# A causal mask added by VectorE in PSUM in place of a TensorE product

## The chip, the cores and the metric

The kernel runs on one core of a Trainium2 chip. The metric is the device time of one execution in microseconds (us). Engines are named as in the profile: PE is TensorE (PEld its weight loads), DVE VectorE, ACT ScalarE, POOL GpSimd, SP SyncE.

## The reference

The reference is a transformer block with adaptive layer norm over two sequences of 1024 positions and 512 channels, in float32. The change touches the attention in it:

```python
q = (x @ Wq).reshape(b, s, H, D).transpose(0, 2, 1, 3)      # H = 32, D = 64
k = (x @ Wk).reshape(b, s, KVH, D).transpose(0, 2, 1, 3)    # KVH = 8
v = (x @ Wv).reshape(b, s, KVH, D).transpose(0, 2, 1, 3)
q, k = apply_rope(q, pos), apply_rope(k, pos)
scores = jnp.einsum('bhqd,bhkd->bhqk', q, k) / jnp.sqrt(jnp.float32(D))
causal = jnp.tril(jnp.ones((s, s), dtype=bool))
scores = jnp.where(causal[None, None], scores, jnp.finfo(x.dtype).min)
attn = jax.nn.softmax(scores, axis=-1)
out = jnp.einsum('bhqk,bhkd->bhqd', attn, v)
```

A layer norm stands in front of it; the output projection, a second layer norm and a gated feed-forward layer with ternary weights stand behind it.

## The kernel before

The kernel has four stages, one behind the other: `prologue` (layer norm), `attention`, `project_outputs` and `feed_forward`. Only `attention` is touched.

Attention runs in 8 groups, one per key-value head with its 4 query heads, and each group in 72 steps. Every product is done with operands split into a high and a low part, to keep float32 accuracy. For each sequence and each query block i of 128 queries, a head's scores against all keys up to the diagonal are one "row": `scores` writes up to 1024 columns into PSUM (two matmuls for each 512 columns, lines 641 and 642), and one more matmul (line 643) of `mask_r` by `ident_r` adds the causal mask of 0 and -1e30 to the last 128 columns, which are the diagonal block. `maximum` (VectorE, line 768) takes the negated maximum of the row, and `exponentials` (ScalarE, line 708) writes the probabilities and their sum. The probabilities are then turned tile by tile: `turn` (four 128x128 transposes on TensorE, line 651), `high` (ScalarE, line 695, writes `p_hi`), `low` (VectorE, line 760, writes `p_lo`), and two steps later `values` (lines 663 and 664) multiplies them by the values.

Query blocks are taken in pairs, a big one of 5 to 8 tiles and a small one of 4 to 1, 9 tiles together. So a pair is 9 steps with one tile each, and the 8 rows of the next pair (4 heads, big and small) are scored in steps 0, 1, 3, 4, 5, 6, 6 and 7 of the nine. Their maxima and exponentials are queued one step later, so in steps 1, 2, 4, 5, 6, 7 (two rows) and 8; steps 0 and 3 have none. The projections of the next queries, keys and values go in between: four steps of matmuls each, then the rotary products on VectorE (lines 783 and 784), a half swap by DMA, a sum on GpSimd, and casts on ScalarE (lines 729, 734, 741, 745).

Each engine's order is written out by hand: a function `step` per engine lists what the engine does in step T. The engines wait for each other by semaphores (`Events`). Scores have four PSUM banks, so `scores` waits for the exponential of a row two to four rows earlier (`ROW_FREED`); `turn` has two banks and waits for the low split of two steps before. Where the program speaks of `body.rows(T, 1)` it means the rows scored one step ago, and `body.tile(T, 0)` is this step's tile.

Of the kernel before, what the change touches and what calls it, by code (L numbers as in the profile page):

```python
# [20 lines left out]
ALU = mybir.AluOpType  # L21
# [3 lines left out]
F32R = mybir.dt.float32r  # L25
BF16 = mybir.dt.bfloat16

P = 128
B, S, E = 2, 1024, 512
T = B * S  # L30
# [297 lines left out]
def attention(nc, wq, wk, wv, consts_in, w_in, w_raw, cos, sin, mask, ident, hT_hi, hT_lo, ot_dram, rden_dram):  # L328
    with ExitStack() as ctx:
# [2 lines left out]

        w_hi = sb("w_hi", [P, CT, WN], F32R)
        w_lo = sb("w_lo", [P, CT, WN], F32R)
        ident_r = sb("ident_r", [P, P], F32R)
        mask_r = sb("mask_r", [P, P], F32R)
        rot_c = sb("rot_c", [P, 2, 512], F32)
        rot_s = sb("rot_s", [P, 2, 512], F32)
        rot_x = sb("rot_x", [P, 2, 512], F32)
# [12 lines left out]
        rd_rows = sb("rd_rows", [GQ * ST, P], F32)  # L352
        ps = ctx.enter_context(nc.psum_tensor("ps_b", [P, 8, 512], F32))

        consts_ready, pads_ready, k_scaled, whi_ready, w_ready = [sem(n) for n in (
            "consts_ready", "pads_ready", "k_scaled", "whi_ready", "w_ready")]
        s_ready, max_ready, p_ready, t_ready, phi_ready, plo_ready, pv_done = [sem(n) for n in (
            "s_ready", "max_ready", "p_ready", "t_ready", "phi_ready", "plo_ready", "pv_done")]
        o_copied, o_added = sem("o_copied"), sem("o_added")
        o_shifted, o_out = [[sem("%s%d" % (n, i)) for i in range(2)] for n in ("o_shifted", "o_out")]  # L360
        x_ready, x_used, vt_ready, khi_ready, k_ready, vhi_ready = [sem(n) for n in (
# [4 lines left out]
        block = ctx.enter_context(nc.Block())  # L366

        rows_s = Events(s_ready, [1] * RB, RB - ROWS_BEFORE)
        rows_m = Events(max_ready, [1] * RB, RB - ROWS_BEFORE)
        rows_p = Events(p_ready, [1] * RB, RB - ROWS_BEFORE)  # L370
        tiles_t, tiles_hi, tiles_lo, tiles_pv = [Events(s, [1] * STEPS, None) for s in (t_ready, phi_ready, plo_ready, pv_done)]
# [196 lines left out]

        @block.tensor
        def _(pe):  # L570
            pe.wait_ge(consts_ready, 2)
            pe.wait_ge(pads_ready, 1)

            def await_x(g, n):
# [46 lines left out]
            def scores(g, r):  # L621
                unit, _, i, h, _, k = row_of(r)
                first = (r // 8 + 1) % 4
                if k == 0 and first == 0:
                    for n in ([7, 9, 10] if unit == 0 else [0, 2, 3]):
                        if X_USES[n][0] == "kv":
                            kv_lo.await_(pe, g, KV.index(n))
                            kv_hi.await_(pe, g, KV.index(n))
                        else:
                            q_place[buf_of(n)].await_(pe, g, QBUF[buf_of(n)].index(n))  # L630
                if k == 0 and first == 2:
                    for n in ([11, 12] if unit == 0 else [4, 5]):
                        buf = buf_of(n)
                        q_place[buf].await_(pe, g, QBUF[buf].index(n) - (len(QBUF[buf]) if unit == 0 else 0))
                rows_p.await_(pe, g, r - ROW_FREED[k])
                nk = (i + 1) * P
                q = q_hl[:, h, i * P:(i + 1) * P]
                for k0 in range(0, nk, 512):
                    n = min(512, nk - k0)
                    bank = S_BANK + ROW_BANK[k] + k0 // 512  # L640
                    pe.matmul(ps[:, bank, 0:n], q, k_hh[:, unit, k0:k0 + n], start=True, stop=False)  # L641
                    ins = pe.matmul(ps[:, bank, 0:n], q, k_l0[:, unit, k0:k0 + n], start=False, stop=(k0 + n < nk))  # L642
                pe.matmul(ps[:, bank, n - P:n], mask_r[:], ident_r[:], start=False, stop=True).then_inc(s_ready, 1)  # L643

            def turn(g, T):
                unit, parity, i, j, column, block_ = tile_of(T)
# [39 lines left out]
        @block.scalar  # L686
        def _(act):
            act.wait_ge(consts_in, 48)
            act.copy(ident_r[:], ident[:]).then_inc(consts_ready, 1)
            act.copy(mask_r[:], mask[:]).then_inc(consts_ready, 1)  # L690

            def high(g, T):
                tiles_t.await_(act, g, T)
                tiles_pv.await_(act, g, T - P_RING)
                act.copy(p_hi[:, T % P_RING, :], ps[:, T_BANK + T % 2, :]).then_inc(phi_ready, 1)  # L695

            def copy_out(g, n):
                pair, small = divmod(n, 2)
                tiles_pv.await_(act, g, 9 * pair + (8 if small else BIG[pair % 4]))
                blocks_out[n % 2].await_(act, g, n // 2 - 1)  # L700
                act.copy(o_sb[:, n % 2, :], ps[:, O_BANK, :]).then_inc(o_copied, 1)  # L701

            def exponentials(g, r):
                unit, parity, i, h, column, k = row_of(r)
                rows_m.await_(act, g, r)
                nk = (i + 1) * P
                s = ps[:, S_BANK:S_BANK + 4, :].rearrange("p b c -> p (b c)")[:, ROW_BANK[k] * 512:ROW_BANK[k] * 512 + nk]
                act.activation(p_32[:, parity, h, column * P:column * P + nk], s, ACT.Exp, bias=negm[:, k:k + 1], scale=1.0,  # L708
                               accum_out=den[:, unit, h, i:i + 1]).then_inc(p_ready, 1)

            def step(body, T):
                if body.split(T, W_HIGH):
                    splits_in.await_(act, body.g, 0)
                    k_cols = w_raw[:, :, GQ * D:GQ * D + D]
                    act.activation(k_cols, k_cols, ACT.Copy, scale=D ** -0.5).then_inc(k_scaled, 1)
                    splits_scaled.await_(act, body.g, 0)
                    uses_x.await_(act, body.g, X_HERE - 1)
                    act.copy(w_hi[:], w_raw[:]).then_inc(whi_ready, 1)
                for g, t in body.tile(T, 0):
                    high(g, t)  # L720
                for g, n in body.blocks(T, LAG):
                    copy_out(g, n)
                for g, r in body.rows(T, 1):
                    exponentials(g, r)
                for g, n, _ in body.uses(T, 4, kinds=("kv",)):
                    buf = buf_of(n)
                    uses_x.await_(act, g, n)
                    await_buffer(act, g, n)
                    act.copy(rot_c[D:P, buf, :], ps[D:P, X_BANK, :]).then_inc(vt_ready, 1)
                for g, n, _ in body.uses(T, 1, kinds=("v",)):  # L730
                    unit = X_USES[n][1]
                    uses_x.await_(act, g, n)
                    tiles_pv.await_(act, g, (36 if unit == 0 else 0) - 1)
                    act.copy(v_hl[:, unit, :, 0:D],
                             ps[:, X_BANK, :].rearrange("p (t d) -> p t d", d=D)).then_inc(vhi_ready, 1)
                for g, n, _ in body.uses(T, 8, kinds=("kv",)):
                    _, unit, part, _ = X_USES[n]
                    buf_sum[part].await_(act, g, BUF[part].index(n))
                    rows_s.await_(act, g, 23 if unit == 0 else (55 if n == X_BODY - 1 else 55 - RB))
                    for rows in half:  # L740
                        act.copy(k_hh[rows, unit, kv_cols(part)], rot_c[0:D, part, :]).then_inc(khi_ready, 1)
                for g, n, _ in body.uses(T, 8, kinds=("qx", "qy")):
                    buf = buf_of(n)
                    buf_sum[buf].await_(act, g, BUF[buf].index(n))
                    act.copy(rot_s[:, buf, :].bitcast(F32R), rot_c[:, buf, :]).then_inc(qhi_ready[buf], 1)
                for g, d in body.dens(T, 0):
                    dens_turned.await_(act, g, d)
                    dens_out.await_(act, g, d - 1)
                    act.copy(rd_rows[:], ps[0:GQ * ST, X_BANK, 0:P]).then_inc(rd_copied, 1)

            bodies(act, step)
# [3 lines left out]
        def _(dve):  # L755
            dve.wait_ge(consts_in, 48)

            def low(g, T):
                tiles_hi.await_(dve, g, T)
                dve.tensor_tensor(p_lo[:, T % P_RING, :], ps[:, T_BANK + T % 2, :], p_hi[:, T % P_RING, :].bitcast(F32),  # L760
                                  ALU.subtract).then_inc(plo_ready, 1)

            def maximum(g, r):
                _, _, i, _, _, k = row_of(r)
                rows_s.await_(dve, g, r)
                nk = (i + 1) * P
                s = ps[:, S_BANK:S_BANK + 4, :].rearrange("p b c -> p (b c)")[:, ROW_BANK[k] * 512:ROW_BANK[k] * 512 + nk]
                dve.tensor_reduce(negm[:, k:k + 1], s, AX.X, ALU.max, negate=True).then_inc(max_ready, 1)  # L768

            def rotary_products(g, n):  # L770
# [15 lines left out]
            def step(body, T):  # L786
                for g, n, _ in body.uses(T, 4, kinds=("kv", "qx", "qy")):
                    await_buffer(dve, g, n)
                    rotary_products(g, n)
                for g, r in body.rows(T, 1):  # L790
                    maximum(g, r)
                for g, n, _ in body.uses(T, 1, kinds=("v",)):
                    unit = X_USES[n][1]
                    v_high.await_(dve, g, V.index(n))
                    dve.tensor_tensor(v_hl[:, unit, :, D:P], ps[:, X_BANK, :].rearrange("p (t d) -> p t d", d=D),
                                      v_hl[:, unit, :, 0:D].bitcast(F32), ALU.subtract).then_inc(x_used, 1)
                for g, t in body.tile(T, 0):
                    low(g, t)
                for g, d in body.dens(T, -1):
                    rows_p.await_(dve, g, 23 if d == 0 else 55)  # L800
                    dens_turned.await_(dve, g, d - 1)
# [727 lines left out]
```

## Time and profile before

| | us |
|---|---|
| median of 3 runs (2105.07 to 2113.36) | 2111.36 |
| the profiled execution | 2113.28 |
| its span, first to last instruction | 2111.5 |
| attention's tiles, first to last split | 1176.4 |

The time of a run has some 2 us around the span. The profile gives each engine's busy time, what ended its idle time ("<-" and the releasing engine and line), and the granted TensorE clock, where 1.00 is 2.4 GHz and a mean between 0.5 and 1 is a mixture with 1.2 GHz. Durations of neighbouring instructions on one engine overlap in their ends, so the step from one start to the next is what an instruction costs in its queue. Line numbers are those of the kernel before.

### The profile page before, as it was taken

Reading aid. Unit: us, or ns where it says so; the run is one execution under the profiler, and the core shown is the slowest. Engines: PE = TensorE matmul, PEld = TensorE weight load, DVE = VectorE, ACT = ScalarE, POOL = GpSimd, SP = SyncE. Lnnn points to the kernel's source line nnn. Section 1 sums busy time; section 2 is a strip of 40 time slices with the busy share of each in tenths; the row PEclk is TensorE's granted clock in tenths of the full one; section 3 lists DMA queues with packets and bytes.
Section 4 is the critical chain, followed back from the end, with each engine's and each line's share of the span. In section 5 each row is a group of like instructions: output and inputs, shape, how many; then the busy total and the mean of one; then the engine's idle time right before and its main releaser. Section 6 shows DMA issues by size and latency. Waiting matters only on the chain. (4 is left out here: it accounts for less than half of the span.)

```text
span 2111.5 us, 30964 instructions
## 1 busy us (share of the span) xinstructions
PE 1808.2 (86%) x9601; PEld 1499.0 (71%) x9601; DVE 1408.7 (67%) x1935; ACT 1161.6 (55%) x2283; POOL 796.9 (38%) x532
## 2 busy tenths in 40 slices
PE   4679999999999999999999999357766669999997
PEld 4458878878878887787788888245555547777776
DVE  5347777767767777767777777487797946454543
ACT  1137777767767777677677678343343334232221
POOL 0023333333333333333333332175665714444443
PEclk9789999999999999999999999778888889999999
DMA  6033233233233333323332332667577510101000
GB/s 236 6 79 75 58 98 93 58 86 89 66 77 89 80 74 81 83 73 74 95 78 64 91 73 56 173 168 175 151 184 161 146 55 1 45 1 45 1 26 20
DMA packets 161113, 178.62 MB, mean 85 GB/s; under 512 B 25265, under 2 KB 112057, under 8 KB 160961
## 3 DMA queue, kind: packets, MB, share of 16 engines
q1 hardware_dynamic: 160960, 176.64, 32.9%
q8 instruction: 89, 1.46, 0.3%
q14 instruction: 64, 0.52, 0.1%
HBM read 79.83 MB, written 25.44 MB: 50 GB/s over the span
## 5 line engine op out<-in xcount | busy, mean ns | idle before, releaser
L760 DVE TENSOR_TENSOR p_lo<-ps_b,p_hi 128x512 fp32r<-128x512 f32 x576 | 396.0, 689 | 207.2 <-ACT p_hi L695 203.0
L695 ACT CAST p_hi<-ps_b 128x512 fp32r<-128x512 f32 x576 | 338.4, 587 | 253.2 <-PE ps_b L651 247.4
L768 DVE TENSOR_REDUCE negm<-ps_b 128x1 f32<-128x640 f32 (+7 forms) x512 | 379.6, 751 | 93.6 <-PE ps_b L643 89.7
L708 ACT ACTIVATE p<-ps_b,negm 128x640 f32<-128x640 f32 (+7 forms) x512 | 382.3, 749 | 67.9 <-DVE negm L768 63.3
L651 PE MATMUL ps_b<-ident,p 128*128 128x128 f32 x2304 | 352.8, 276 | 14.4 <-issue 8.7
L641 PE MATMUL ps_b<-k_hh,q_hl 128*128 128x512 f32 (+3 forms) x768 | 267.7, 349 | 16.8 <-DMA q_hl<-rot_x 12.1
L651 PEld LDWEIGHTS ps_b<-ident,p 128*128 128x128 f32 x2304 | 251.3, 141 | 41.4 <-issue 13.8
L663 PE MATMUL ps_b<-p_hi,v_hl 128*128 128x512 f32 x576 | 275.8, 479 | 1.7 <-ACT o_sb L701 1.3
L822 POOL TENSOR_TENSOR rot_c<-rot_c,rot_x 128x512 f32<-128x512 f32 (+1 forms) x96 | 123.3, 1285 | 358.1 <-DMA rot_x<-rot_s 358.1
L642 PE MATMUL ps_b<-k_l,q_hl 128*128 128x512 f32 (+3 forms) x768 | 257.0, 347 | 0.0
L977 PE MATMUL ps_c<-wo_hi,o_hi 128*128 128x512 f32 x256 | 120.4, 470 | 139.3 <-DVE o_lo L1115 139.3
L664 PE MATMUL ps_b<-p_lo,v_hl 128*128 128x512 f32 x576 | 227.9, 396 | 0.0
L817 POOL TENSOR_TENSOR o_sb<-o_sb,o_low 64x512 f32<-64x512 f32 x128 | 163.9, 1283 | 147.1 <-DMA o_low<-o_sb 147.0
L1268 PE MATMUL ps_d<-h_hi,gu 128*128 128x512 f32 x512 | 201.3, 393 | 7.8 <-ACT xn_d L1287 4.6
L1269 PE MATMUL ps_d<-h_lo,gu 128*128 128x512 f32 x512 | 200.0, 391 | 0.0
L599 PE MATMUL ps_b<-hT_hi,w_hi 128*128 128x512 f32 x384 | 157.1, 409 | 38.5 <-DVE w_lo L805 13.2
L641 PEld LDWEIGHTS ps_b<-k_hh,q_hl 128*128 128x128 f32 x768 | 145.1, 189 | 57.9 <-issue 16.9
L977 PEld LDWEIGHTS ps_c<-wo_hi,o_hi 128*128 128x128 f32 x256 | 57.9, 226 | 159.0 <-DVE o_lo L1115 90.4
L642 PEld LDWEIGHTS ps_b<-k_l,q_hl 128*128 128x128 f32 x768 | 145.4, 189 | 28.0
L600 PE MATMUL ps_b<-hT_hi,w_lo 128*128 128x512 f32 x384 | 153.6, 400 | 0.0
L601 PE MATMUL ps_b<-hT_lo,w_hi 128*128 128x512 f32 x384 | 152.2, 396 | 0.0
L1436 DVE TENSOR_TENSOR a<-ps_d,sg 128x512 f32<-128x512 f32 x64 | 44.2, 691 | 158.5 <-PE ps_d L1269 140.8
(141 smaller groups left out, 3420.9 us busy)
## 6 DMA issues: line engine op xcount, KB each, us to landing
rot_x<-rot_s SPq DMA_DIRECT2D x320, 64.0 KB, 2.0
q_hl<-rot_s SPq DMA_DIRECT2D x128, 128.0 KB, 2.3
q_hl<-rot_x SPq DMA_DIRECT2D x128, 128.0 KB, 2.4
o_low<-o_sb SPq DMA_DIRECT2D x128, 128.0 KB, 2.2
attention_out<-o_sb SPq DMA_DIRECT2D x128, 128.0 KB, 2.5
o_raw<-attention_out SPq DMA_DIRECT2D x32, 512.0 KB, 4.9
rd<-attention_out SPq DMA_DIRECT2D x64, 256.0 KB, 9.0
wf<-in_L_ffn_w_gate_up SPq DMA_DIRECT2D x16, 512.0 KB, 11.6
```

What stands on the lines that cost most here:

```text
L641: pe.matmul(ps[:, bank, 0:n], q, k_hh[:, unit, k0:k0 + n], start=True, stop=False)
L642: ins = pe.matmul(ps[:, bank, 0:n], q, k_l0[:, unit, k0:k0 + n], start=False, stop=(k0 + n < nk))
L651: ins = pe.transpose(ps[:, T_BANK + T % 2, h * P:(h + 1) * P], p_32[:, parity, h, column * P:(column + 1) * P], ident[:])
L663: pe.matmul(ps[:, O_BANK, :], v_hl[:, unit, j, :], p_hi[:, T % P_RING, :], start=(j == 0), stop=False)
L664: pe.matmul(ps[:, O_BANK, :], v_hl[:, unit, j, :], p_lo[:, T % P_RING, :], start=False, stop=(j == i)).then_inc(pv_done, 1)
L695: act.copy(p_hi[:, T % P_RING, :], ps[:, T_BANK + T % 2, :]).then_inc(phi_ready, 1)
L708: act.activation(p_32[:, parity, h, column * P:column * P + nk], s, ACT.Exp, bias=negm[:, k:k + 1], scale=1.0, accum_out=den[:, unit, h, i ...
L760: dve.tensor_tensor(p_lo[:, T % P_RING, :], ps[:, T_BANK + T % 2, :], p_hi[:, T % P_RING, :].bitcast(F32), ALU.subtract).then_inc(plo_read ...
L768: dve.tensor_reduce(negm[:, k:k + 1], s, AX.X, ALU.max, negate=True).then_inc(max_ready, 1)
L977: pe.matmul(ps[:, i, t, :], hi, wo_hi[:, kk, :], start=(kk == 0), stop=False)
L1268: pe.matmul(ps[:, bank + half, :], gu[:, m, half, k, :], h_hi[:, parity, k, :], start=(k == 0), stop=False)
L1269: i = pe.matmul(ps[:, bank + half, :], gu[:, m, half, k, :], h_lo[:, parity, k, :], start=False, stop=(k == CT - 1))
```

## The change

The mask product on TensorE goes, with its constants `mask_r` and `ident_r`. The second score matmul of a row now ends the accumulation and signals. VectorE adds the mask to the diagonal block in PSUM (`hide_later_keys`), signals `masked`, and `maximum` waits for that signal. In VectorE's step the mask additions stand first, then the low split, and the maxima behind the low split, where they stood ahead of it. The mask constant is turned, as it is added directly now. Nothing else in any engine's order differs.

```diff
-                    ins = pe.matmul(ps[:, bank, 0:n], q, k_l0[:, unit, k0:k0 + n], start=False, stop=(k0 + n < nk))
-                pe.matmul(ps[:, bank, n - P:n], mask_r[:], ident_r[:], start=False, stop=True).then_inc(s_ready, 1)
+                    ins = pe.matmul(ps[:, bank, 0:n], q, k_l0[:, unit, k0:k0 + n], start=False, stop=True)
+                ins.then_inc(s_ready, 1)
...
-            act.copy(ident_r[:], ident[:]).then_inc(consts_ready, 1)
-            act.copy(mask_r[:], mask[:]).then_inc(consts_ready, 1)
...
+            def hide_later_keys(g, r):
+                nk, k, s = row_scores(r)
+                rows_s.await_(dve, g, r)
+                dve.tensor_tensor(s[:, nk - P:nk], s[:, nk - P:nk], mask[:], ALU.add).then_inc(masked, 1)
+
             def maximum(g, r):
-                rows_s.await_(dve, g, r)
+                nk, k, s = row_scores(r)
+                rows_masked.await_(dve, g, r)
                 dve.tensor_reduce(negm[:, k:k + 1], s, AX.X, ALU.max, negate=True).then_inc(max_ready, 1)
...
                 for g, r in body.rows(T, 1):
+                    hide_later_keys(g, r)
+                for g, t in body.tile(T, 0):
+                    low(g, t)
+                for g, r in body.rows(T, 1):
                     maximum(g, r)
...
-                for g, t in body.tile(T, 0):
-                    low(g, t)
```

On VectorE, beside a pair whose next rows are 6 and 3 tiles wide, steps 2 to 5 of the nine stood so before (`negm` is the negated maximum, `rot_c` and `rot_s` the rotary products):

```order
 L760 TENSOR_TENSOR p_lo<-ps_b,p_hi 128x512 [waits b_phi_ready] x2
 L783 TENSOR_TENSOR rot_c<-ps_b,cos 128x512 [waits b_x_ready,b_k_ready]
 L784 TENSOR_TENSOR rot_s<-ps_b,sin 128x512
 L768 TENSOR_REDUCE negm<-ps_b 128x1 [waits b_s_ready]
 L760 TENSOR_TENSOR p_lo<-ps_b,p_hi 128x512 [waits b_phi_ready]
 L768 TENSOR_REDUCE negm<-ps_b 128x1 [waits b_s_ready]
 L760 TENSOR_TENSOR p_lo<-ps_b,p_hi 128x512 [waits b_phi_ready]
```

And so they stand in the changed kernel, in the same place, from step 3:

```order
 L755 TENSOR_TENSOR p_lo<-ps_b,p_hi 128x512 [waits b_phi_ready]
 L786 TENSOR_TENSOR rot_c<-ps_b,cos 128x512 [waits b_x_ready,b_k_ready]
 L787 TENSOR_TENSOR rot_s<-ps_b,sin 128x512
 L766 TENSOR_TENSOR ps_b<-ps_b,mask 128x128 [waits b_s_ready]
 L755 TENSOR_TENSOR p_lo<-ps_b,p_hi 128x512 [waits b_phi_ready]
 L771 TENSOR_REDUCE negm<-ps_b 128x1 [waits b_masked]
 L766 TENSOR_TENSOR ps_b<-ps_b,mask 128x128 [waits b_s_ready]
 L755 TENSOR_TENSOR p_lo<-ps_b,p_hi 128x512 [waits b_phi_ready]
 L771 TENSOR_REDUCE negm<-ps_b 128x1 [waits b_masked]
```

The low split moved from behind the maximum to between the mask addition and the maximum. ScalarE's queue in the changed kernel, steps 4 to 7 of the same nine, is the same as before but for the line numbers (each CAST of `p_hi` is `high`, each ACTIVATE an exponential):

```order
 L703 ACTIVATE p,den<-ps_b,negm 128x768 [waits b_max_ready]
 L690 CAST p_hi<-ps_b 128x512 [waits b_pv_done,b_t_ready]
 L703 ACTIVATE p,den<-ps_b,negm 128x768 [waits b_max_ready]
 L690 CAST p_hi<-ps_b 128x512 [waits b_pv_done,b_t_ready]
 L703 ACTIVATE p,den<-ps_b,negm 128x384 [waits b_max_ready]
 L690 CAST p_hi<-ps_b 128x512 [waits b_pv_done,b_t_ready]
```

Nothing moved in that queue; what moved is the work that `b_max_ready` stands for.

## Rows read from the trace of the kernel before

**Rows 1.** The page: 40 slices, PE's busy tenths and granted clock.

```profile
PE   4679999999999999999999999357766669999997
...
PEclk9789999999999999999999999778888889999999
```

**Rows 2.** Stretches: length, busy PE, PEld, DVE, ACT, POOL, PEclk, DMA share, GB/s.

```profile
147.20:1323.60 1176.40, 1120.28 (x6666) 951.46 (x6663) 865.98 (x1297) 867.08 (x1905) 389.95 (x306) 1.00 0.32 78
...
1420.00:1500.00 80.00, 58.90 (x237) 45.41 (x235) 65.86 (x44) 31.39 (x32) 50.17 (x20) 0.82 0.72 174
```

**Rows 3.** Waits from 147 to 1324 us: total us, times, longest.

```profile
ACT p_hi L695 <- PE ps_b L651: 247.0, 276, 4.4
...
DVE p_lo L760 <- ACT p_hi L695: 203.0, 326, 2.2
...
DVE negm L768 <- PE ps_b L643: 77.6, 129, 3.2
...
PE ps_b L641 <- ACT p L708: 2.6, 9, 0.3
```

**Rows 4.** PE in order of time: start us, duration us, line, operation.

```profile
703.02 0.22 PE L643 MATMUL ps_b<-ident_r,mask_r 128*128 128x128 f32 x1
703.08 0.39 PE L641 MATMUL ps_b<-k_hh,q_hl 128*128 128x384 f32 x1
...
709.38 0.28 PE L643 MATMUL ps_b<-ident_r,mask_r 128*128 128x128 f32 x1
709.49 0.62 PE L651 MATMUL ps_b<-ident,p 128*128 128x128 f32 x4
```

**Rows 5.** DVE and then ACT in order of time, same columns, with idle before.

```profile
700.73 0.95 DVE L768 TENSOR_REDUCE negm<-ps_b 128x1 f32<-128x768 f32 x1
...
702.19 0.55 DVE L768 TENSOR_REDUCE negm<-ps_b 128x1 f32<-128x384 f32 x1
703.21 0.69 DVE L760 TENSOR_TENSOR p_lo<-ps_b,p_hi 128x512 fp32r<-128x512 f32 x1 [0.47 <-ACT p_hi L695]
703.82 1.01 DVE L768 TENSOR_REDUCE negm<-ps_b 128x1 f32<-128x384 f32 x2
...
701.71 0.90 ACT L708 ACTIVATE p<-ps_b,negm 128x768 f32<-128x768 f32 x1 [0.73 <-DVE negm L768]
...
702.60 0.58 ACT L695 CAST p_hi<-ps_b 128x512 fp32r<-128x512 f32 x1
703.07 0.59 ACT L708 ACTIVATE p<-ps_b,negm 128x384 f32<-128x384 f32 x1
```

**Rows 6.** DVE groups by shape, 147.2 to 1323.6 us: busy, mean ns, idle before.

```profile
L768 DVE TENSOR_REDUCE negm<-ps_b 128x1 f32<-128x512 f32 x64 | 42.5, 685 | 5.7 <-PE ps_b L643 5.1
...
L783 DVE TENSOR_TENSOR rot_c<-ps_b,cos 128x512 f32<-128x512 f32 x60 | 41.0, 683 | 0.1
...
L768 DVE TENSOR_REDUCE negm<-ps_b 128x1 f32<-128x128 f32 x60 | 16.6, 287 | 4.1 <-PE ps_b L643 1.7
```

**Rows 7.** Groups by line, same stretch, same columns.

```profile
L708 ACT ACTIVATE p<-ps_b,negm 128x896 f32<-128x896 f32 (+3 forms) x504 | 376.4, 750 | 53.9 <-DVE negm L768 49.5
L768 DVE TENSOR_REDUCE negm<-ps_b 128x1 f32<-128x896 f32 (+3 forms) x504 | 373.7, 751 | 81.3 <-PE ps_b L643 77.6
...
L643 PE MATMUL ps_b<-ident_r,mask_r 128*128 128x128 f32 x504 | 119.3, 237 | 0.0
...
L745 ACT CAST rot_s<-rot_c 128x512 fp32r<-128x512 f32 x60 | 37.2, 620 | 0.0
L741 ACT CAST k_hh<-rot_c 64x512 fp32r<-64x512 f32 x60 | 37.0, 617 | 0.7
L729 ACT COPY rot_c<-ps_b 64x512 f32<-64x512 f32 x30 | 17.5, 582 | 0.7
...
L718 ACT CAST w_hi<-w_raw 128x1536 fp32r<-128x1536 f32 x7 | 10.4, 1482 | 0.7
L734 ACT CAST v_hl<-ps_b 128x512 fp32r<-128x512 f32 x15 | 8.8, 588 | 0.0
```

More of the change, by code:

```diff
@@ L334, in attention @@
         w_lo = sb("w_lo", [P, CT, WN], F32R)
-        ident_r = sb("ident_r", [P, P], F32R)
-        mask_r = sb("mask_r", [P, P], F32R)
         rot_c = sb("rot_c", [P, 2, 512], F32)
@@ L353, in attention @@
         ps = ctx.enter_context(nc.psum_tensor("ps_b", [P, 8, 512], F32))
[L355 to L358, printed above, removed]
+        pads_ready, k_scaled, whi_ready, w_ready = [sem(n) for n in ("pads_ready", "k_scaled", "whi_ready", "w_ready")]
+        masked, s_ready, max_ready, p_ready, t_ready, phi_ready, plo_ready, pv_done = [sem(n) for n in (
+            "masked", "s_ready", "max_ready", "p_ready", "t_ready", "phi_ready", "plo_ready", "pv_done")]
         o_copied, o_added = sem("o_copied"), sem("o_added")
@@ L368, in attention @@
         rows_s = Events(s_ready, [1] * RB, RB - ROWS_BEFORE)
+        rows_masked = Events(masked, [1] * RB, RB - ROWS_BEFORE)
         rows_m = Events(max_ready, [1] * RB, RB - ROWS_BEFORE)
@@ L570, in _ @@
         def _(pe):
-            pe.wait_ge(consts_ready, 2)
             pe.wait_ge(pads_ready, 1)
@@ L761, in low, with row_scores @@
                                   ALU.subtract).then_inc(plo_ready, 1)
+            def row_scores(r):
+                _, _, i, _, _, k = row_of(r)
+                nk = (i + 1) * P
+                return nk, k, ps[:, S_BANK:S_BANK + 4, :].rearrange("p b c -> p (b c)")[:, ROW_BANK[k] * 512:ROW_BANK[k] * 512 + nk]
+            def hide_later_keys(g, r):
+                nk, k, s = row_scores(r)
+                rows_s.await_(dve, g, r)
+                dve.tensor_tensor(s[:, nk - P:nk], s[:, nk - P:nk], mask[:], ALU.add).then_inc(masked, 1)
             def maximum(g, r):
-                _, _, i, _, _, k = row_of(r)
-                rows_s.await_(dve, g, r)
-                nk = (i + 1) * P
-                s = ps[:, S_BANK:S_BANK + 4, :].rearrange("p b c -> p (b c)")[:, ROW_BANK[k] * 512:ROW_BANK[k] * 512 + nk]
+                nk, k, s = row_scores(r)
+                rows_masked.await_(dve, g, r)
                 dve.tensor_reduce(negm[:, k:k + 1], s, AX.X, ALU.max, negate=True).then_inc(max_ready, 1)
@@ L1519 @@
     arrays = {"in_" + name: np.ascontiguousarray(inputs[name]) for name in INPUTS}
-    arrays.update(in_cos=cos, in_sin=sin, in_mask=np.where(k > q, np.float32(NEG), np.float32(0)).astype(np.float32),
+    arrays.update(in_cos=cos, in_sin=sin, in_mask=np.where(k < q, np.float32(NEG), np.float32(0)).astype(np.float32),
                   in_identity=np.eye(P, dtype=np.float32))
```

## The prediction

> **What bounds the kernel now.** I first read the page's slices, to find the stage. The mask is used in the attention stage alone, where TensorE shows nine tenths and more in slice after slice at a full granted clock [rows 1]. The stretch between the first and the last split of a probability tile is 1176.4 us long, with 576 such tiles, so 2.04 us each; TensorE is busy for 1120.3 us of it, VectorE for 866.0 and ScalarE for 867.1 [rows 2]. Matmul durations overlap, so the busy time doesn't prove that TensorE is dense; the waits do. ScalarE waits 247.0 us for the transposes of TensorE, VectorE waits 203.0 us for ScalarE's split and 77.6 us for the mask product, while TensorE waits for a softmax row only 2.6 us [rows 3]. Everyone waits for TensorE. A TensorE slot saved in this stage is therefore worth its full length, as long as the other two keep their slack. Whether they keep it is the whole question.
>
> **What is removed.** 512 mask products leave TensorE (504 of them in the stretch). Their mean duration is 237 ns, but that is mostly pipeline. The start of one to the start of the next matmul is 0.06 us behind a wide score product and 0.11 us behind a 128-wide one [rows 4]. So the path gains 504 x 0.06 = 30 us to 504 x 0.11 = 55 us, no more, and not the 119 us of its busy row. The two constant casts on ScalarE and the wait for them lie ahead of the stage, under other work: nothing.
>
> The Trainium skill (TensorE: Matmul & The Clock Gate, Back-to-back issue gap) gives a warm gap of N / 2.4 + 2.5 ns, which is 56 ns for 128 columns. The first of the two slots agrees, and the estimate by it alone would be 29 us for the whole gain, 2 us short of the low end.
>
> **What is added.** 512 additions of 128x128 on VectorE, one input in PSUM. The trace has none of this size. The nearest row is the 128-wide reduction from PSUM, 287 ns; the 512-wide PSUM operation, 683 ns, is the other bound [rows 6]. I take 0.29, since the width is the same, and 0.21 us of queue, because neighbours on VectorE overlap by 0.08 (a low split of 0.69 us is followed by the next start after 0.61 [rows 5]). That is 504 x 0.21 = 106 us more VectorE work, 972 of 1176. As work it fits under TensorE.
>
> **What is moved.** This is the step that decides. For an attention step T the changed queues hold:
> ScalarE: split high(T), then the exponentials of the rows scored in step T-1, then its casts for the projections, then high(T+1).
> VectorE: mask of those rows, split low(T), then the row maxima, then step T+1.
> Before, the maxima stood ahead of low(T). A maximum ran while ScalarE did high(T), and low(T) ran under the exponential; neither queue waited for the other twice in one step. The slack is seen at 702.60: high(T) is followed by its exponential after 0.47 us, because the maximum had started at 702.19, before low(T) [rows 5].
> Now low(T) waits for high(T), the maximum stands behind low(T), the exponential waits for the maximum, and high(T+1) stands behind the exponential on ScalarE. Queued behind the waiting low split are the maximum, and through it the exponential, the next high split and the next low split. It is a ring through both engines, once per step with rows, and nothing in it overlaps.
>
> **The ring, term by term.** Eight score rows per nine steps fall in seven of them (one step has two), so the stretch has 63 x 7 = 441 steps with rows and 135 plain ones.
> 1. Start of high to start of low: 702.60 to 703.21, 0.61 us [rows 5]. 441 x 0.61 = 269 us.
> 2. Start of low to start of the maximum behind it: 703.21 to 703.82, 0.61 us [rows 5]. 269 us. The mask's own semaphore is long set, since low lies between.
> 3. Maximum to exponential: the row sum 373.7 us [rows 7] and 0.03 us of hand-over each (700.73 + 0.95 to 701.71 [rows 5]), 389 us. In 63 steps the second row's maximum hides under the first exponential; such small rows cost from 0.29 to 0.69 us [rows 6], say 0.52 with the hand-over: -33. So 356 us.
> 4. Exponential to high: row sum 376.4 us [rows 7]; the accumulator read lies inside (701.71 to 702.60 is 0.89 for one of 0.90 [rows 5]), less 0.02 each: 366 us.
> 5. Plain steps: low split 0.61 and mask 0.21 on VectorE run in series there, about 0.81. 135 x 0.81 = 109 us. Without that pairing it would be ScalarE's 0.47: 63 us.
> 6. ScalarE's other casts, 37.2 + 37.0 + 17.5 + 10.4 + 8.8 = 111 us [rows 7], stand in its queue between an exponential and the next high. Most fall behind steps with rows: 100 us. Were they all hidden: 0.
> 7. The rotary products, two of 0.68 us [rows 6] or 1.2 us of queue, hide under exponential and high, which together are longer, except directly behind a plain step (four uses a group, 32): 38 us.
> The sum is 269 + 269 + 356 + 366 + 109 + 100 + 38 = 1507 us for a stretch that took 1176: 331 us more. The mask itself lies beside the ring (VectorE waits there for high anyway) and costs nothing except in term 5; the copies of the output stand between high and the exponential, under low and the maximum.
> TensorE needs 1176 - 43 = 1133 us for its own work, which now hides under 1507. It is asked in time: a transpose needs the low split of two steps before, and a score row needs the exponential of one or two steps before, which is at least 2 us ahead of its use in the ring. Its saved slots bring nothing.
> The profiled execution took 2113.3 us around a span of 2111.5, 2 us over the median shown. 2113 + 331 = 2444, and some 6 us for the value splits, which wait for a ScalarE copy and then stand ahead of the next mask: **2450 us**, 16% slower.
>
> The Trainium skill (VectorE: DVE Perf Modes, The DRAIN you can't avoid) says that the next operation does not start until the pipe is empty. The 0.61 us above speaks against it for these operations, and the same page's section on two instructions with no wait between them allows it. With full durations of 0.69 term 2 would be an estimate of 304 us and the time some 2485.
>
> **The rivals.**
> A, faster: the ring's period stays under TensorE's. This would need the queues to overlap low(T) with an exponential of the same step, or a period below 2.04 us. For it: VectorE and ScalarE are idle a quarter of the time [rows 2], and the added work fits. Against it: one ring step with an average row is 0.61 + 0.61 + 0.77 + 0.73 = 2.7 us, and the plain steps give back only 1.2 us each, 162 us against 441 x 0.7 = 309. If it holds: 2113 less 30 to 55, **2058 to 2083**.
> B, the product's slot doesn't go away: the weight load of the transposes takes it, and A holds otherwise: **2113**.
> C, the ring closes, but its soft terms hide: 5 at 63, 6 and 7 at nothing, 1323 us in all, +147: **2260**; with half of them, 2350. For it: casts that wait for the projections might find the ring waiting anyway.
> D, TensorE can't run ahead through the plain steps. They would then cost its own 2.04 us and not 0.81: 135 x 1.23 = +166, **2610**. It decides if a transpose is late whenever two short ring steps meet. Against it: behind the low split that frees the transposes' bank the ring still has a maximum and an exponential, while TensorE needs under 1 us.
> E, the granted clock falls. TensorE is 74% busy from 1420 to 1500 us, about the share it would have in the ring, and there the clock was 0.82 [rows 2]. At such a mean 36% of the time is at 1.2 GHz, where nine steps need 2 x 18 = 36 us of TensorE against the ring's 23.9: 9 steps take 1 / (0.36 / 36 + 0.64 / 23.9) = 27 us, 1720 in all, **2660**. Against it: that stage has long waits for data, while here each wait is under 2 us, and the attention stage ran at 1.00 throughout.
>
> **How the numbers follow.** The ring as summed 0.63, C 0.10, D 0.12, E 0.08, A 0.05, B 0.02. The likeliest gives 2450. To hold 8 in 10 the range takes the ring with its bounds, the upper half of C and D: 2320 to 2630; A, B, the rest of C and most of E are left out. Faster by over 0.5% is A, 0.05; within 0.5%, which is about what a measurement here can't tell from no change, B, 0.02; slower the rest, 0.93.
>
> **What would show it.** In the changed profile the stretch of the tiles should be near 1507 us; VectorE's low split still waits for ScalarE's high; above all ScalarE's exponential should wait for the maximum some 441 times and over 1.2 us each time with big rows (49.5 us in total now [rows 7]), which is several hundred us. TensorE should wait for exponentials and low splits, hundreds of us where there are hardly any. The idle before the score reductions should be near nothing. The maximum's start should lie 0.61 us behind the low split's. The mask addition should be 0.29 us. The clock at 1.00 decides against E, and a stretch of under 1176 us with the exponential close behind high(T) would refute the ring. I am wrong in size rather than sign if transposes turn up as the releaser of high(T) behind plain steps (D), or if casts run while VectorE is the later one (C).

## The result

| | median, us | ratio to before | 95% interval |
|---|---|---|---|
| before | 2112.4 | | |
| changed | 2491.9 | 1.181 | 1.178 to 1.183 |

The change makes the kernel 18% slower: 380 us more, where 2450 us had been forecast in a range of 2320 to 2630. The loss lies in attention alone. Its tiles take 1557.8 us, from the start of the first low split to the start of the last, against 1176.4 [rows 2]; everything behind them takes 783 us, and took some 787.

The stretch of the tiles, to the end of its last split, and the rest in the changed kernel (length, then busy PE, PEld, DVE, ACT, POOL, PEclk, DMA share, GB/s):

```profile
145.10:1703.60 1558.50, 1223.54 (x6162) 957.43 (x6160) 964.12 (x1801) 865.89 (x1905) 393.93 (x307) 0.93 0.24 59
...
1703.60:2486.00 782.40, 608.21 (x2594) 483.95 (x2594) 471.48 (x501) 262.60 (x322) 387.68 (x209) 0.89 0.35 91
```

ScalarE does exactly the work that it did (865.9 us busy, 867.1 before) in 382 us more. VectorE is busy for 98 us more, with 504 mask additions. No engine is full. What fills the time is seen in the waits of the same stretch (total us, times, longest), which answer to [rows 3]:

```profile
ACT p L703 <- DVE negm L771: 633.6, 441, 3.1
DVE p_lo L755 <- ACT p_hi L690: 554.7, 458, 2.4
...
PE ps_b L638 <- ACT p L703: 145.9, 125, 3.0
...
ACT p_hi L690 <- PE ps_b L648: 45.1, 50, 3.0
PE ps_b L616 <- DVE rd_b L807: 44.9, 15, 3.6
...
ACT p_hi L690 <- PE ps_b L661: 8.4, 3, 2.9
```

ScalarE's exponentials wait for a maximum 441 times, once in every step with rows, for 634 us (49.5 before, in [rows 7]); VectorE's low split waits 555 us for ScalarE's high split. The two engines wait for each other in turn, and TensorE, for which both used to wait, waits for them: ScalarE's wait for the transposes fell from 247 to 45 us.

One step of that, ACT and then DVE in order of time (start us, duration us, line, operation, idle before):

```profile
801.74 0.58 ACT L690 CAST p_hi<-ps_b 128x512 fp32r<-128x512 f32 x1
803.67 0.69 ACT L703 ACTIVATE p<-ps_b,negm 128x512 f32<-128x512 f32 x1 [1.35 <-DVE negm L771]
804.26 0.19 ACT L703 ACTIVATION_READ_ACCUMULATOR p<-ps_b,negm 128x1 f32 x1
804.35 0.58 ACT L690 CAST p_hi<-ps_b 128x512 fp32r<-128x512 f32 x1
...
802.35 0.69 DVE L755 TENSOR_TENSOR p_lo<-ps_b,p_hi 128x512 fp32r<-128x512 f32 x1 [1.22 <-ACT p_hi L690]
802.96 0.68 DVE L771 TENSOR_REDUCE negm<-ps_b 128x1 f32<-128x512 f32 x1
803.56 0.49 DVE L766 TENSOR_TENSOR ps_b<-ps_b,mask 128x128 f32<-128x128 f32 x2
804.96 0.69 DVE L755 TENSOR_TENSOR p_lo<-ps_b,p_hi 128x512 fp32r<-128x512 f32 x1 [0.92 <-ACT p_hi L690]
```

High starts at 801.74, low at 802.35, the maximum at 802.96, the exponential at 803.67, the next high at 804.35: 0.61 + 0.61 + 0.71 + 0.68 = 2.61 us, one behind the other. The two mask additions at 803.56 lie in VectorE's idle time, under the exponential.

### The profile page after: what moved, and what is told of

Same layout as the page of the kernel before. It is cut to its first block and busy times, and to the rows that moved or that the text cites. A ratio compares the mean times of both kernels' runs of the same rounds, so it can differ in the third digit from the quotient of the medians.

```text
span 2486.4 us, 30451 instructions
## 1 busy us (share of the span) xinstructions
PE 1914.7 (77%) x9089; PEld 1505.7 (61%) x9089; DVE 1499.9 (60%) x2447; ACT 1159.9 (47%) x2281; POOL 798.9 (32%) x532
## 5 line engine op out<-in xcount | busy, mean ns | idle before, releaser
L638 PE MATMUL ps_b<-k_hh,q_hl 128*128 128x512 f32 (+3 forms) x768 | 293.5, 382 | 158.3 <-ACT p L703 147.7
L648 PE MATMUL ps_b<-ident,p 128*128 128x128 f32 x2304 | 382.1, 292 | 40.8 <-ACT rot_c L724 17.3
L690 ACT CAST p_hi<-ps_b 128x512 fp32r<-128x512 f32 x576 | 329.4, 583 | 54.9 <-PE ps_b L648 45.1
L648 PEld LDWEIGHTS ps_b<-ident,p 128*128 128x128 f32 x2304 | 291.7, 150 | 99.9 <-issue 35.7
L660 PE MATMUL ps_b<-p_hi,v_hl 128*128 128x512 f32 x576 | 294.0, 510 | 59.0 <-ACT o_sb L696 58.0
L639 PE MATMUL ps_b<-k_l,q_hl 128*128 128x512 f32 (+3 forms) x768 | 271.4, 366 | 0.0
L661 PE MATMUL ps_b<-p_lo,v_hl 128*128 128x512 f32 x576 | 239.9, 417 | 0.0
L838 POOL TENSOR_TENSOR rot_x<-rot_c,rot_s 128x512 fp32r<-128x512 f32 x64 | 82.2, 1284 | 393.2 <-ACT rot_s L740 393.2
L639 PEld LDWEIGHTS ps_b<-k_l,q_hl 128*128 128x128 f32 x768 | 155.9, 203 | 27.0
L660 PEld LDWEIGHTS ps_b<-p_hi,v_hl 128*128 128x128 f32 x576 | 118.3, 205 | 74.8 <-ACT o_sb L696 73.9
L766 DVE TENSOR_TENSOR ps_b<-ps_b,mask 128x128 f32<-128x128 f32 x512 | 142.4, 289 | 26.5 <-PE ps_b L639 25.4
```

Of the source, the lines that this page charges most:

```text
L648: ins = pe.transpose(ps[:, T_BANK + T % 2, h * P:(h + 1) * P], p_32[:, parity, h, column * P:(column + 1) * P], ident[:])
L660: pe.matmul(ps[:, O_BANK, :], v_hl[:, unit, j, :], p_hi[:, T % P_RING, :], start=(j == 0), stop=False)
L661: pe.matmul(ps[:, O_BANK, :], v_hl[:, unit, j, :], p_lo[:, T % P_RING, :], start=False, stop=(j == i)).then_inc(pv_done, 1)
```

## The experiments

Two explanations were to be told apart: the ring (the order of VectorE's queue, with the low split ahead of the maxima), and the mask's own work and wait on VectorE. After the first runs a third question came up, what the addition costs in a queue without the ring. Each edit is against the kernel that is named; ratios are to the kernel before, with 95% intervals.

### The order without the mask addition

Against the kernel before, mask product still on TensorE:

```diff
                 for g, n, _ in body.uses(T, 4, kinds=("kv", "qx", "qy")):
                     await_buffer(dve, g, n)
                     rotary_products(g, n)
+                for g, t in body.tile(T, 0):
+                    low(g, t)
                 for g, r in body.rows(T, 1):
                     maximum(g, r)
...
-                for g, t in body.tile(T, 0):
-                    low(g, t)
```

> The kernel before with its mask product on TensorE, but VectorE's maxima queued behind the low split, as in the changed kernel; no mask addition. The theory of the ring (high, low, maximum, exponential, high in series through ScalarE and VectorE) expects nearly the whole loss: the changed kernel's 2492 us less the mask's share of plain steps (126 x 0.21 = 26) and no more, so 2455 to 2500 us, with ScalarE waiting some 600 us for maxima. The rival, that the mask addition on VectorE is the cost (504 x 0.29 = 146 us of work and its wait), expects 2105 to 2160 us.

Measured: 2484.0 us, ratio 1.176 (1.170 to 1.182). The order alone brings the whole loss but for 8 us, which the two intervals don't separate; the kernel has no addition on VectorE at all. The 26 us that the mask was to cost in plain steps are not seen. The waits have the same pattern:

```profile
DVE p_lo L760 <- ACT p_hi L695: 679.6, 470, 4.0
ACT p L708 <- DVE negm L768: 619.5, 443, 2.9
```

### The mask addition without the order

Against the changed kernel, the low split goes back behind the maxima:

```diff
                     hide_later_keys(g, r)
-                for g, t in body.tile(T, 0):
-                    low(g, t)
                 for g, r in body.rows(T, 1):
                     maximum(g, r)
...
+                for g, t in body.tile(T, 0):
+                    low(g, t)
                 for g, d in body.dens(T, -1):
```

> The changed kernel with the low split moved back behind the maxima: the mask is added by VectorE, and the maximum follows it at once and waits for it. The ring theory expects the kernel to be bound by TensorE again and to gain the slots of the mask product, 30 to 55 us: 2058 to 2090 us. The rival that the mask addition or the maximum's wait for it is the cost expects 2150 us or more, up to the changed kernel's 2492.

Measured: 2138.8 us, ratio 1.013 (1.009 to 1.018). The ring is gone with the order: 353 us of the loss of 380. The two waits of the ring have shrunk with it:

```profile
ACT p L703 <- DVE negm L771: 140.1, 234, 2.4
DVE p_lo L755 <- ACT p_hi L690: 124.3, 182, 1.1
```

But neither theory had this number right. The kernel is not faster than before by the product's slots but 26 us slower, which the runs further down take apart.

### The addition doubled, beside the ring and in it

Against the changed kernel, each row's mask is added a second time, with a semaphore of its own for which the maximum waits. In the first kernel the second addition stands ahead of the low split, in the second behind it:

```diff
                 for g, r in body.rows(T, 1):
                     hide_later_keys(g, r)
+                for g, r in body.rows(T, 1):      # first kernel
+                    hide_again(g, r)
                 for g, t in body.tile(T, 0):
                     low(g, t)
+                for g, r in body.rows(T, 1):      # second kernel
+                    hide_again(g, r)
                 for g, r in body.rows(T, 1):
                     maximum(g, r)
```

> The changed kernel with the mask added twice to each row (each addition with a semaphore of its own; -2e30 masks as well as -1e30), both additions ahead of the low split. On the ring theory VectorE waits there for ScalarE's high split anyway, so only the steps behind a plain one pay, 126 x 0.35 = 44 us at most: 2500 to 2545 us. The rival that work on VectorE sets the time expects 512 x 0.35 = 180 us more: 2640 to 2680 us.

Measured: 2517.1 us, ratio 1.194 (1.188 to 1.199): 25 us over the changed kernel, for 512 more operations of 0.29 us.

> The same second addition, but behind the low split and ahead of the maximum. Now it stands in the ring: 504 x 0.21 = 106 us over the changed kernel, 2580 to 2620 us. The rival that only the amount of VectorE work counts expects the same time as with both additions ahead of the low split.

Measured: 2661.2 us, ratio 1.261 (1.254 to 1.267): 169 us over the changed kernel, for the same 512 operations. The place decides: seven times the price two lines further down. The size was put too low. In the 378 steps with one row the second addition and the maximum that waits for it are neighbours there, and from the start of the one to the start of the other takes 0.32 us, not 0.21 (shown below). In the 63 steps with two rows another addition lies between, and each takes 0.20. That is 378 x 0.32 + 126 x 0.20 = 146 us; the stretch of the tiles grew by 160 (1718.1 against 1557.8). The other 14 us are open.

### More work for TensorE in the ring

Against the changed kernel, the first score matmul of each bank is issued twice:

```diff
+                    pe.matmul(ps[:, bank, 0:n], q, k_hh[:, unit, k0:k0 + n], start=True, stop=True)
                     pe.matmul(ps[:, bank, 0:n], q, k_hh[:, unit, k0:k0 + n], start=True, stop=False)
```

> The changed kernel with the first score matmul of each bank issued twice (the first closes a sum, the second starts it anew, so the result is the same). It adds some 768 slots of up to 0.22 us, about 130 us of TensorE work, to attention. If the ring alone sets the pace, the work hides and the granted clock rises: 2485 to 2525 us. If TensorE's lateness in the ring (53 us of ScalarE's waits) is a matter of its work, more than half of the added work shows: 2560 us or more.

Measured: 2518.8 us, ratio 1.192 (1.189 to 1.195). Of some 130 us of added work, as forecast (TensorE's busy time in the stretch grew by 104), 27 us show; the rest hides under the ring. The granted clock rose from 0.93 to 0.95. The high split's wait for TensorE grew from 45.1 + 8.4 = 53.5 us to 79.7, by about as much as the time:

```profile
ACT p L704 <- DVE negm L772: 626.7, 443, 3.1
ACT p_hi L691 <- PE ps_b L649: 79.7, 70, 3.6
```

So TensorE is not the bound in the ring, but not wholly beside it either.

### What the mask product's slot is worth

Against the kernel before, the product is left out and nothing takes its place, so this kernel leaves out the causal mask:

```diff
-                pe.matmul(ps[:, bank, n - P:n], mask_r[:], ident_r[:], start=False, stop=True).then_inc(s_ready, 1)
+                ins.then_inc(s_ready, 1)
```

> The kernel before without its mask product, and nothing in its place (the causal mask is left out). It measures what the product's slot on TensorE is worth by itself: 30 to 55 us, 2058 to 2083 us. The rival, that the slot is taken by the weight load of the next matmul, expects 2105 to 2115 us. Against e2_mask_only (2139) the difference is what the addition costs on VectorE in its best-looking place.

Measured: 2090.9 us, ratio 0.991 (0.988 to 0.993). The slot is worth 19 to 22 us, less than the 30 to 55 forecast. The slots themselves do go. Before, the transposes started 0.11 us behind the product [rows 4], and the product behind the last score matmul. Here they start 0.11 us behind the last score matmul itself:

```profile
700.89 0.28 PE L642 MATMUL ps_b<-k_l,q_hl 128*128 128x128 f32 x1
701.00 0.62 PE L651 MATMUL ps_b<-ident,p 128*128 128x128 f32 x4
```

The whole stretch (length, then busy PE and the rest as in [rows 2]):

```profile
150.00:1301.10 1151.10, 1082.15 (x6162) 899.69 (x6160) 860.95 (x1297) 866.59 (x1905) 389.61 (x306) 1.00 0.33 80
```

TensorE's busy time fell from 1120.3 to 1082.2 us, by 38 us, which lies within the 30 to 55. But the stretch fell by 25 only, since TensorE's idle time rose from 56.1 to 69.0 us. A part of the 13 us is seen in its waits for the copies to `rot_c` (12.4 us where there were 8.3) and for the exponentials (5.2 where there were 2.6 [rows 3]):

```profile
PE ps_b L651 <- ACT rot_c L729: 7.2, 13, 0.9
PE ps_b L599 <- ACT rot_c L729: 5.2, 7, 0.8
PE ps_b L641 <- ACT p L708: 5.2, 13, 0.5
```

So the slots were priced rightly, and a third of what they free is lost again to idle time.

### What the addition costs without the ring

Against the kernel with the mask addition and the old order, the sum is written to a tile that nobody reads, so these kernels leave out the causal mask too. In the first one the maximum doesn't wait for the addition, in the second it does:

```diff
-                dve.tensor_tensor(s[:, nk - P:nk], s[:, nk - P:nk], mask[:], ALU.add).then_inc(masked, 1)
+                dve.tensor_tensor(beside[:, k], s[:, nk - P:nk], mask[:], ALU.add)                       # first
+                dve.tensor_tensor(beside[:, k], s[:, nk - P:nk], mask[:], ALU.add).then_inc(masked, 1)   # second
...
-                rows_masked.await_(dve, g, r)
+                rows_s.await_(dve, g, r)                                                                 # first
```

> e2_mask_only with the VectorE addition written to a tile that nobody reads, and the maximum waiting for the scores alone (so the causal mask is left out). The addition costs its slot, 0.21 us, but no wait of the maximum for it. If what e2 loses against e3_no_mask (48 us) is VectorE's queue becoming longer, two thirds of it remain: 2110 to 2130 us. If it is all the maximum's wait for the mask, nothing remains: 2085 to 2100 us.

Measured: 2111.6 us, ratio 0.999 (0.997 to 1.001).

> As e9_beside_no_wait, but the maximum waits for the addition, as in e2_mask_only (the causal mask is left out). Slot 0.33 us. Writing to SBUF in place of PSUM should matter little: 2130 to 2145 us, as e2. A lower time would say that writing into the score bank has a price of its own.

Measured: 2137.9 us, ratio 1.011 (1.008 to 1.014), the same as with the sum in place (2138.8). So the write into the score bank costs nothing of its own. From the kernel without a mask (2091) the addition's place in the queue costs 18 to 21 us, and the maximum's wait for its neighbour 26 us more. The two queues, DVE in order of time, first without the wait and then with it:

```profile
701.56 0.28 DVE L767 TENSOR_TENSOR beside<-ps_b,mask 128x128 f32<-128x128 f32 x1
701.75 0.95 DVE L772 TENSOR_REDUCE negm<-ps_b 128x1 f32<-128x768 f32 x1
```

```profile
703.77 0.28 DVE L767 TENSOR_TENSOR beside<-ps_b,mask 128x128 f32<-128x128 f32 x1
704.09 0.96 DVE L772 TENSOR_REDUCE negm<-ps_b 128x1 f32<-128x768 f32 x1
```

That is 0.19 us from start to start without the wait, 0.32 with it; over both traces the medians are 0.20 and 0.32. The longer step is found 378 times in the stretch and not 504: in steps with two rows both additions come first, and the maximum starts 0.20 us behind the second one even where it waits. So the addition takes 378 x 0.32 + 126 x 0.20 = 146 us of VectorE's queue, of which the waits are 378 x 0.12 = 45. Both engines behind TensorE had slack on average, yet not in every step: these 146 us cost 47 us of time.

### The low split of the step before

The changed kernel hides the maximum's wait for the mask under a low split. Taking the split of the step before would keep that and open the ring. First in the changed kernel, then, as a control, in the kernel before with the product on TensorE, where the split is moved ahead of the maxima as well:

```diff
-                for g, t in body.tile(T, 0):
+                for g, t in body.tile(T, 1):
                     low(g, t)
```

> The changed kernel in its own order (mask, low split, maxima), but the low split taken is that of the step before. Its high split then stands ahead of the exponential that ran beside it, so no ring closes within a step, and the low split between mask and maximum hides the wait for the mask. The ring theory expects TensorE to bind again: 2058 to 2110 us. If instead a low split between mask and maximum were harmful by itself, or VectorE's amount of work the bound, 2139 us (as e2) or more.

Measured: 2155.0 us, ratio 1.023 (1.020 to 1.025). The ring is open (in the stretch ScalarE waits 164 us for maxima and not 634), but the forecast of 2058 to 2110 us was missed, and this is worse than the old order with the same addition (2138.8).

> The kernel before, mask product on TensorE, with the low split of the step before placed ahead of the maxima. The control to e6: the ring is open and TensorE has its old work, so 2100 to 2125 us. A gain or loss here of over 1% would belong to the shift and not to the mask.

Measured: 2130.1 us, ratio 1.011 (1.008 to 1.014), a little over the forecast. The shift itself costs 20 us: the transposes need the low split of two steps before, and now wait for it more. In the kernel before TensorE's wait for it was 0.9 us, or up to 9.6 with waits for which the profile names no releaser; in the control and in the shifted changed kernel it is

```profile
PE ps_b L651 <- DVE p_lo L760: 18.2, 22, 2.3
```

```profile
PE ps_b L648 <- DVE p_lo L755: 31.7, 69, 1.4
```

These waits cover a part of the cost only: in the control all of TensorE's idle time grew by 8 us (from 56.1 to 64.4), while the stretch grew by 14. The rest is open.

### Small rows on VectorE, big rows on TensorE

The old order, and only the rows with k of 4 and over (the small ones) masked by VectorE; for the others the product stays:

```diff
+                if k < 4:
+                    ins = pe.matmul(ps[:, bank, n - P:n], ident_r[:], mask_r[:], start=False, stop=True)
                 ins.then_inc(s_ready, 1)
```

> The order of e2_mask_only, but only the four small rows of a pair are masked by VectorE, where its maxima are short, and the four big ones keep the product on TensorE. Half of e3's gain of 19 us without the crowding of VectorE in the steps with big rows: 2095 to 2112 us. If VectorE's queue is full in the small steps as well (one of them has two rows), it gains nothing: 2112 to 2130 us.

Measured: 2103.5 us, ratio 0.996 (0.994 to 0.998). It computes the whole block and is the fastest such version here, by 0.4%, which is at the edge of what can be told.

## Why the prediction was right, and where it was off

**The bound before.** Held: everyone waited for TensorE, but with less room behind it than the averages say. Leaving the product out brought 19 to 22 us, not 30 to 55. The slots were priced rightly (38 us less busy time), which also answers rival B: they do go. What failed is that a saved slot "is worth its full length": 13 us of what was saved became new idle time of TensorE, and half of that are waits for ScalarE's copies and exponentials.

**The ring.** Held, and shown by four runs: the order alone makes the loss (2484), the addition without it doesn't (2139), and an operation is nearly free ahead of the low split (25 us) and costly behind it (169 us). The profile has the sign that was named above all: 441 waits for maxima, once for each step with rows. Of TensorE's waits half of what was named came: those for the exponentials are 145.9 us, but those for the low split 13.4, not hundreds.

**The terms.** High to low 0.61, low to maximum 0.61 and maximum to exponential its duration plus 0.03 were read again to the hundredth. The addition is 289 ns, where 0.29 was taken:

```profile
L766 DVE TENSOR_TENSOR ps_b<-ps_b,mask 128x128 f32<-128x128 f32 x504 | 140.0, 289 | 14.4 <-PE ps_b L639 13.4
```

**The size.** The ring was summed to 1507 us and took 1557.8. The starts in the trace of the changed kernel, added up over all its steps, show which terms held:

| part of the ring | forecast, us | measured, us |
|---|---|---|
| high to low, with the rotary products (terms 1, 7) | 307 | 317.6 |
| low to maximum (2) | 269 | 267.2 |
| maximum to exponential (3) | 356 | 361.0 |
| exponential to next high, plain steps, casts (4, 5, 6) | 575 | 558.5 |
| ScalarE's high split waiting for TensorE | none | 53.7 |

The step that was mis-sized is the sentence that TensorE "is asked in time". The high split waited for TensorE for 53.7 us (of these 45.1 for transposes and 8.4 for value products in the waits above), which no term contained; the other parts together are within 3 us of their forecast. Rival C, by which the soft terms hide, did not hold: the casts and the plain steps count almost in full. Of the 53.7 us, 38.6 stand in plain steps and 14.3 at the starts of five groups. They come at places that recur in each group. One is the transpose of the denominators: its reciprocal stands behind the maxima on VectorE, and so now behind the ring. PE, ACT and DVE there, in the changed kernel:

```profile
916.08 0.34 DVE L807 RECIPROCAL rd_b<-den 128x32 f32<-128x32 f32 x1
...
916.55 0.39 PE L616 MATMUL ps_b<-ident,rd_b 128*32 128x128 f32 x1 [3.05 <-DVE rd_b L807]
916.66 0.79 PE L638 MATMUL ps_b<-k_hh,q_hl 128*128 128x512 f32 x1
...
917.67 0.63 PE L638 MATMUL ps_b<-k_hh,q_hl 128*128 128x512 f32 x1
...
918.10 0.63 PE L639 MATMUL ps_b<-k_l,q_hl 128*128 128x512 f32 x1
...
918.53 1.05 PE L648 MATMUL ps_b<-ident,p 128*128 128x128 f32 x4
...
919.62 0.59 ACT L690 CAST p_hi<-ps_b 128x512 fp32r<-128x512 f32 x1 [1.60 <-PE ps_b L648]
```

TensorE waits 3.05 us for the reciprocal. Then its 512-wide matmuls start 0.43 us apart (917.67 to 918.10) instead of 0.23 (822.66 to 822.89, shown in the last section), which is the lower of its two clock levels, and the next high split waits 1.60 us. Such places, one in each group, where lateness and clock mostly meet, make 10.7 of the 53.7 us; by the clock record about 23 us end at the lower level and the rest at the full one. So rival D (transposes late at plain steps) came true in a small measure, 39 us where it had 166, and rival E (the clock) had a smaller part in it: the granted clock of the stretch was 0.93, where it had been 1.00. That these waits are the missing 51 us is argued from the trace; no run took them away, and the parts can hide one another. The control with more TensorE work supports it, since there the wait for TensorE and the time grew together, by 26 and 27 us.

**The rest.** Rival A (faster) fell to the order. Its number would have been wrong as well: even with the old order the addition loses 26 us, since the sum took 106 us of added queue where it is 146 with the waits, and took an average of slack for slack in each step. Behind the low split, as changed, that wait was indeed covered. The estimate with full durations, by the Trainium skill (VectorE: DVE Perf Modes, The DRAIN you can't avoid), came to 2485 by chance: the 0.61 us that speaks against it stood in the changed kernel too (term 2 measured 267 us, not 304).

## What to carry to other kernels

When two in-order engines hand work to each other within a step, follow one item through both queues and back before moving an instruction: if each engine's next item stands behind its partner's answer, the durations add up, and neither engine looks full. Average slack is not slack in every step; here 146 us of work put into 310 us of VectorE's idle time cost 47. Where work can be given to either of two engines, it may pay to split it by size, and to give each the instances for which it has room; here that brought 0.4%, and why it did was not tested further.

## What the runs showed of the hardware

A wait of a VectorE instruction for the one right before it costs 0.12 us (0.32 against 0.20 us from start to start, medians), in the 378 rows where the two are neighbours some 45 us of queue; with another instruction between, as in the 126 rows of steps with two, it costs nothing. The Trainium skill (VectorE: DVE Perf Modes, The DRAIN you can't avoid) states that "the semaphore costs nothing extra here" for a row of copies; on this pair the measurement differs, and it decides.

A 128-wide product of TensorE, whose busy row says 237 ns, took 0.076 us of TensorE's busy time with it when it was taken away (38.1 us for 504), and was worth 0.05 us (25.3 us of the tiles' stretch).

A single wait of TensorE of about 3 us can be followed by the lower clock level, but need not be. Behind the wait of 3.05 us at 916.55 matmuls ran at the lower level. Behind one of 2.78 us in the same kernel, PE in order of time, they start 0.23 us apart, the full level:

```profile
821.97 0.28 PE L616 MATMUL ps_b<-ident,rd_b 128*32 128x128 f32 x1 [2.78 <-DVE rd_b L807]
...
822.66 0.40 PE L638 MATMUL ps_b<-k_hh,q_hl 128*128 128x512 f32 x1
822.89 0.39 PE L639 MATMUL ps_b<-k_l,q_hl 128*128 128x512 f32 x1
```

And behind a shorter one, of 2.45 us before a transpose at 857.05, the granted clock fell from 1.00 to 0.50 at 857.73. What decides between them these runs don't show.
